# Masked attention layer on one core: exponentials and sums of four heads at a time, three denominator terms, transposes moved, batches written out

## The reference

```python
h = jnp.maximum(_layernorm(x, axis=-1), 0.0)          # x: 8 x 1024 x 512
q = heads(h @ Wq + bq); k = heads(h @ Wk + bk); v = heads(h @ Wv + bv)   # 16 heads of 32
scores = jnp.einsum('bhqd,bhkd->bhqk', q, k) / sqrt(32)
scores = jnp.where(adj[:, None] == 0, -jnp.inf, scores)
attn = jax.nn.softmax(scores, axis=-1)
out = jnp.einsum('bhqk,bhkd->bhqd', attn, v).transpose(0, 2, 1, 3).reshape(8, 1024, 512)
return x + out @ Wo + bo
```

## Time and profile before

| | |
|---|---|
| median of 3 runs | 2086.7 us (2085.78 to 2088.95) |
| profiled execution, its own time / its span | 2085.51 / 2083.6 us |
| TensorE busy | 1932.5 us, 93% |
| VectorE busy | 1557.3 us, 75% |
| ScalarE busy | 1478.1 us, 71% |
| POOL busy | 1302.1 us, 62% |
| granted TensorE clock, mean | 0.989 |
| DMA | 206.61 MB, mean 99 GB/s, the program's queue 35.2% of 16 engines |

### The profile page before, as it was taken

The page is one execution under the profiler, slowest core; times in us unless marked ns, Lnnn a source line. Parts: engine busy times, 40 slices in busy tenths (PEclk is TensorE's granted clock), DMA queues, the critical chain, the costliest instruction groups (busy, mean ns, idle before and its releaser), DMA issues.

```text
span 2083.6 us, 40441 instructions
## 1 busy us (share of the span) xinstructions
PE 1932.5 (93%) x14336; PEld 776.5 (37%) x14336; DVE 1557.3 (75%) x1587; ACT 1478.1 (71%) x1765; POOL 1302.1 (62%) x581
## 2 busy tenths in 40 slices
PE   3799899998999999999999999999899998999977
PEld 2334344343344333443334333334333343444312
DVE  5688777878768787687867877778767787767773
ACT  3577786677867788668876778767777677866672
POOL 0377567556666567656667557666557566676574
PEclk8999999999999999999999999999999999999999
DMA  5433244342444324343351434424234332442302
GB/s 177 122 87 96 82 112 132 88 107 64 120 112 124 83 76 132 86 122 86 92 142 56 115 93 117 119 74 119 81 109 122 88 106 66 117 122 64 74 1 81
DMA packets 103222, 206.61 MB, mean 99 GB/s; under 512 B 11616, under 2 KB 11744, under 8 KB 103008
## 3 DMA queue, kind: packets, MB, share of 16 engines
q1 hardware_dynamic: 103008, 203.80, 35.2%
HBM read 153.43 MB, written 50.33 MB: 98 GB/s over the span
## 4 chain that ended last, share of the span: by engine, by line
PE 76%; DVE 7%; issue 6%; DMA 5%; ACT 2%; POOL 1%; SPq 1%; DVEq 0%; ACTq 0%; POOLq 0%
PE ps L694 20%; PE ps L681 19%; PE ps L654 15%; PE ps L705 10%; PE ps L668 7%; PE ps L661 6%; DVE ring L905 4%; DMA k_stack<-k_parts 2%; DMA k_parts<-k_part 1%; SPq L513 1%; DMA edges<-adjT 1%; ACT hT_hi L776 1%; DVE k_part L918 1%; POOL acc L1079 1%; ACT ring L770 1%
## 5 line engine op out<-in xcount | busy, mean ns | idle before, releaser
L905 DVE TENSOR_TENSOR ring<-ps,mask 128x1024 f32<-128x1024 f32 x1024 | 1234.6, 1219 | 435.7 <-PE ps L681 399.9
L770 ACT ACTIVATE ring<-ring 128x1024 f32<-128x1024 f32 x1024 | 1069.7, 1051 | 382.9 <-DVE ring L905 374.6
L1079 POOL TENSOR_TENSOR acc<-ring 128x1024 f32<-128x1024 f32 x256 | 604.1, 2371 | 730.2 <-ACT ring L770 729.4
L681 PE MATMUL ps<-q_stack,k_stack 128*128 128x512 f16 x2048 | 610.4, 382 | 85.2 <-DVE ring L905 61.4
L1079 POOL TENSOR_TENSOR acc<-acc,ring 128x1024 f32<-128x1024 f32 x256 | 617.6, 2432 | 0.0
L694 PE MATMUL ps<-ring,v_sb 128*32 128x512 f32 x4096 | 509.1, 604 | 0.0
L681 PEld LDWEIGHTS ps<-q_stack,k_stack 128*128 128x128 f16 x2048 | 157.1, 98 | 481.8 <-DVE ring L905 246.4
L694 PEld LDWEIGHTS ps<-ring,v_sb 128*32 128x32 f32 x4096 | 100.9, 109 | 252.3 <-issue 218.1
L705 PE MATMUL ps<-acc,ones 128*32 128x512 f32 x1024 | 139.8, 597 | 2.7 <-issue 2.6
L705 PE MATMUL ps<-ring,ones 128*32 128x512 f32 x1024 | 137.3, 592 | 0.0
L661 PE MATMUL ps<-wv_hi,hT_hi 128*128 128x128 f16 x1024 | 103.1, 219 | 3.2 <-DVE k_part L918 3.2
(11 more groups left out here) (80 smaller groups left out, 1593.4 us busy)
## 6 DMA issues: line engine op xcount, KB each, us to landing
x_in<-x SPq DMA_DIRECT2D x168, 256.0 KB, 2.7
edges<-adjT SPq DMA_DIRECT2D x128, 256.0 KB, 2.9
q_stack<-q_parts SPq DMA_DIRECT2D x128, 256.0 KB, 4.9
k_stack<-k_parts SPq DMA_DIRECT2D x128, 256.0 KB, 5.0
q_parts<-q_part SPq DMA_DIRECT2D x32, 512.0 KB, 2.7
k_parts<-k_part SPq DMA_DIRECT2D x32, 512.0 KB, 2.9
out<-x_in SPq DMA_DIRECT2D x56, 256.0 KB, 2.1
ring<-x SPq DMA_DIRECT2D x2, 1024.0 KB, 6.6
```

Of the source, the lines that this page charges most:

```text
L681: i = nc.tensor.matmul(ps_s(j)[:, hh, :], stack["k"][:, up % 2, h, kt * P:(kt + 1) * P], stack["q"][:, up % 2, h, half * HALF:(half + 1) * ...
L770: nc.scalar.activation(tile, tile, ACT.Exp, scale=SCALE / UP / UP).then_inc(s["prob_ready"], 1)
L905: nc.vector.tensor_tensor(ring[:, slot_of(kt, pair), :].rearrange("p (a n) -> p a n", n=HALF), ps_s(j), mask[:, kt:kt + 1, half * HALF:(ha ...
L1079: nc.gpsimd.tensor_tensor(acc[:, group, pair, :], first_of, ring[:, slot_of(kt, pair), :], ALU.add).then_inc(s["sum_done"], 1)
```

## The change

Five things are done at once.

1. Exponentials: `exp` does nothing for the first tile of a pair and takes both tiles, 128 x 2048, at the second.
2. Sums: POOL adds 128 x 2048 at a time. Group A is now key tiles 0 to 3, group B 4 to 6: five adds in a sweep, at key tiles 1, 2, 3, 5 and 6. Each add within a group waits for the add before it.
3. Denominators: three terms, A, B and d7. BLOCKS has them at other places: nothing at tile 16 (the next sweep's 0), and p6, dB, p7, d7 all at 18 (the next sweep's 2).
4. Chunks: T_AT is gone. The transposes stand in the lists, t0 to t3 between the chunks of unit 2 and t4 to t7 between those of unit 3, and everything is spread over SLOTS, which now has tile 16. In both units the order is q0, k0, v0 and then q1, k1, v1. Laid out, k's second chunk ends at tile 23 in unit 2 (before 11), at 24 in unit 3 (before 20), and at 21 in unit 1 (before 23).
5. Batches 1 to 6 are written out as straight code on all five engines.

```diff
-BLOCKS = {6: ("p0", "p1"), 10: ("p2", "p3", "dA"), 14: ("p4", "p5"), 16: ("p6", "dB", "d6"), 18: ("p7", "d7")}
-TERMS = "AB67"
+BLOCKS = {6: ("p0", "p1"), 10: ("p2", "p3"), 14: ("p4", "p5", "dA"), 18: ("p6", "dB", "p7", "d7")}
+TERMS = "AB7"
+
+SUMMED = {1: 0, 2: 1, 3: 2, 5: 3, 6: 4}
+SUMS = 5
+SUMMED_AT = {"A": 3, "B": 5}
...
-NORMALISE_AT = {(2, 5): 0, (2, 7): 1, (2, 9): 2, (2, 11): 3, (2, 23): 4, (2, 25): 5, (2, 27): 6, (2, 29): 7}
-T_AT = {(2, 19): 0, (2, 21): 1, (2, 23): 2, (2, 25): 3, (2, 27): 4, (2, 29): 5, (3, 1): 6, (3, 3): 7}
-SLOTS_OF = [SLOTS, SLOTS, [j for j in SLOTS if j <= 17], [j for j in SLOTS if j >= 5]]
-NORMS_AT = [29, 29, 18, 29]
+NORMALISE_AT = {(2, 5): 0, (2, 7): 1, (2, 9): 2, (2, 11): 3, (2, 21): 4, (2, 25): 5, (2, 29): 6, (3, 2): 7}
+NORMS_AT = 29
...
     if up == UNITS - 1:
-        return [] if last else ts + PROJ + [NORMS]
+        return [] if last else [q[0], ts[4], k[0], *ts[5:8], v[0], q[1], k[1], v[1], NORMS]
     if up == 2:
-        return PROJ + [NORMS] + ts
+        if last:
+            return [q[0], k[0], v[0], q[1], k[1], v[1], NORMS]
+        return [q[0], k[0], v[0], ts[0], q[1], ts[1], k[1], ts[2], v[1], ts[3], NORMS]
...
             graph(0, True, False)
-            with pe.Fori(1, B - 1) as b:
+            for b in range(1, B - 1):
                 graph(b, False, False)
...
             def exp(U, j):
-                half, r = divmod(j, SWEEP)
+
+                kt, pair = divmod(j % SWEEP, PAIRS)
+                if pair != PAIRS - 1:
+                    return
                 act.wait_ge(s["score_masked"], U * TILES + j + 1)
-                tile = ring[:, slot_of(*divmod(r, PAIRS)), :]
+                tile = ring[:, slot_of(kt, 0):slot_of(kt, 0) + PAIRS, :]
                 nc.scalar.activation(tile, tile, ACT.Exp, scale=SCALE / UP / UP).then_inc(s["prob_ready"], 1)
...
-                if kt < RING_KT:
-                    if not very_first:
-                        if kt < 2:
-                            dve.wait_ge(s["pv_done"], 8 * V + kt - 3)
-                            dve.wait_ge(s["sum_done"], 8 * V + 2 * kt - 3 + pair)
-                        else:
-                            dve.wait_ge(s["den_done"], len(TERMS) * V + kt - 3)
-                else:
-                    dve.wait_ge(s["pv_done"], 8 * V + kt - 3)
-                    dve.wait_ge(s["sum_done"], 8 * V + {4: 1, 5: 1, 6: 3, 7: 5}[kt] + pair)
+                before = (V - 1, kt + QT - RING_KT) if kt < RING_KT else (V, kt - RING_KT)
+                if not (kt < RING_KT and very_first):
+                    W, k = before
+                    dve.wait_ge(s["pv_done"], QT * W + k + 1)
+                    if k == QT - 1:
+                        dve.wait_ge(s["den_done"], len(TERMS) * (W + 1))
+                    else:
+                        dve.wait_ge(s["sum_done"], SUMS * W + SUMMED[k if k in SUMMED else k + 1] + 1)
...
-            def sums(U, j, very_first):
-                half, r = divmod(j, SWEEP)
-                kt, pair = divmod(r, PAIRS)
+            def sums(U, half, kt, very_first):
                 V = U * SWEEPS + half
-                group, k = divmod(kt, 3)
-                pool.wait_ge(s["prob_ready"], U * TILES + j + 1)
-                if k == 1 and pair == 0 and not very_first:
+                group, n = kt // 4, SUMS * V + SUMMED[kt]
+                pool.wait_ge(s["prob_ready"], V * QT + kt + 1)
+                begins = kt % 4 == 1
+                if begins and not very_first:
                     pool.wait_ge(s["den_done"], len(TERMS) * (V - 1) + group + 1)
-                if k == 2:
-                    pool.wait_ge(s["sum_done"], 8 * V + 4 * group + pair + 1)
-                first_of = ring[:, slot_of(kt - 1, pair), :] if k == 1 else acc[:, group, pair, :]
-                nc.gpsimd.tensor_tensor(acc[:, group, pair, :], first_of, ring[:, slot_of(kt, pair), :], ALU.add).then_inc(s["sum_done"], 1)
+                if not begins:
+                    pool.wait_ge(s["sum_done"], n)
+                tile = ring[:, slot_of(kt, 0):slot_of(kt, 0) + PAIRS, :]
+                first_of = ring[:, slot_of(kt - 1, 0):slot_of(kt - 1, 0) + PAIRS, :] if begins else acc[:, group]
+                nc.gpsimd.tensor_tensor(acc[:, group], first_of, tile, ALU.add).then_inc(s["sum_done"], 1)
```

More of the change, by code:

```diff
@@ L879, in _ @@
             graph(0, True, False)
-            with act.Fori(1, B - 1) as b:
+            for b in range(1, B - 1):
                 graph(b, False, False)
@@ L1040, in _ @@
             graph(0, True, False)
-            with dve.Fori(1, B - 1) as b:
+            for b in range(1, B - 1):
                 graph(b, False, False)
@@ L1099, in graph @@
                                     bias_x(b, first, b - 1, t)
-                        if j % SWEEP // PAIRS in (1, 2, 4, 5):
-                            sums(U, j, first and up == 0 and j < SWEEP)
+                        half, r = divmod(j, SWEEP)
+                        kt, pair = divmod(r, PAIRS)
+                        if pair == PAIRS - 1 and kt in SUMMED:
+                            sums(U, half, kt, first and up == 0 and half == 0)
             pool.wait_ge(s["const_loaded"], 16 * 6)
             graph(0, True, False)
-            with pool.Fori(1, B - 1) as b:
+            for b in range(1, B - 1):
                 graph(b, False, False)
```

95 lines of the change are left out of this document (41 added, 54 removed).

## The result

| | before | after |
|---|---|---|
| median of 4 runs, us | 2087.82 (2085.78 to 2091.12) | 2204.66 (2200.73 to 2208.41) |
| ratio, 95% interval | | 1.0558 (1.0532 to 1.0584): slower |
| profiled execution / its span, us | 2085.51 / 2083.6 | 2208.41 / 2206.6 |
| granted TensorE clock, mean | 0.989 | 0.964 |

The forecast was 2079, with 2045 to 2122 as its range. The result, 2205, is 117 us slower than before and lies outside. The five parts cost more than any of the rivals had them cost.

What follows compares the result with a forecast made beforehand. A ring of waits through POOL's sums was to bind the light units at 28.9 us a sweep, TensorE unit 1. Batch and end terms totalled -7.8 on 2085.5, giving 2077.7; with 1.2 for the median, 2079, range 2045 to 2122.

Steps and rivals of the forecast that it cites:

- The adds: POOL's sums of 2048 elements: 4.54 us each, bounds 4.49 and 4.74.
- The ring: Reciprocal, exponential of key tile 1, POOL's five sums, dB and d7 wait in a circle: 28.9 us a sweep in light units.
- the sign that I had named: If right, 28.9 us from logarithm to logarithm in units 2 and 3.
- Unit 0's first sweep: 28.9 us plus 1.0 and four bias adds of 1.25 between POOL's sums: 34.9 us.
- Written out: The loop's jump back goes five times, 3.3 us each: 17 us saved with the tails, longer program costed at nothing.
- Fewer terms and empty tiles: TensorE: one denominator term fewer, -1.9 us a unit; tiles with nothing but scores, +1.1 at each of 31 unit borders.
- This makes ScalarE lighter by ... 100 us, worth nothing by itself: ScalarE is 2% of the chain: Exponentials of 2048 at 1.9 us each on ScalarE: 100 us less work, no time gained by itself.
- Such a pair of adds took 5.70 us instead of 4.70 ... +1.0 in each unit but unit 1.: First sweep of a unit: VectorE's low part of the attention output falls on a POOL add, +1.0 us except unit 1.
- I count some 14 us from k's end to the next unit against 12.5 ... 0, bounds 0 and 2 per unit.: Ends of units 2 and 3: k's later end was to cost no wait for the k stack, with 1.1 us slack.
- Bank waits ... 0.4 in unit 2: q, k and v waiting for banks behind the short transposes: 0.4 us in unit 2, bounds 0 and 1.8.
- B: Rival: POOL adds of 4.74 us between key tiles 1 and 6 slow the ring, 2128 us; chance 0.18.
- A: Rival: TensorE stays the bound because the ring opens, batch 239.7 us, whole 2009 us; chance 0.12.

Runs made afterwards that it cites:

- a_recip: The changed kernel with ScalarE's reciprocal one tile later, behind the exponential of key tile 1: 2172.46 us.
- b_longexp: b_unroll with exponentials of 2048 only, POOL's eight adds of 1024 kept: 2135.95 us.
- b_long: b_unroll with exponentials and adds of 2048, four adds a sweep, four terms, old chunks: 2165.57 us.
- b_longadd: b_unroll with the four adds of 2048 only, exponentials of one pair kept: 2096.23 us.
- a_olow: The changed kernel with the attention output of units 2 and 3 split at tiles 17 and 19, in POOL's pause, not 5 and 7: 2166.11 us.
- b_long_olow: b_long with the output split of units 2 and 3 moved as in a_olow: 2127.60 us.
- b_chunks16: b_unroll with the new chunk order and slots alone, four terms, pieces of 1024: 2171.14 us.
- b_unroll: The kernel before with batches 1 to 6 written out as straight code, nothing else: 2074.64 us.
- a_kfirst: The changed kernel with q1 and k1 before v0 in unit 3, so k ends at tile 20 instead of 24: 2209.80 us.
- b_three: b_unroll with three terms at their new places and ten adds of 1024, exponentials of 1024, old chunks: 2041.92 us.
- b_best: b_three with the moves of a_recip and a_olow: 2031.07 us.

## Why the prediction was wrong, step by step

**Right.** The adds: 4.54 forecast, 4.563 measured for those that open a group, 4.549 in a_recip; the Trainium skill's 4497 ns for 2048 elements ("GPSIMD Engine Reference", section 3.1) agrees within 1.5%. The ring: from the logarithm in unit 1's second sweep to the one in unit 2's first it took 29.2 us in every batch, 28.9 forecast, and opening it brought 32 us, net of the low part's shift. But the sign that I had named, 28.9 from logarithm to logarithm in units 2 and 3, did not show: from there on these stretches took 30.8 to 38.6 us in batches 1 to 6, so other waits were added to the ring there or took its place. Unit 0's first sweep took 34.9 between its logarithms, as forecast; but b_longexp has 67.5 us for its unit 0 without that ring, so unit 0's sum is no proof of its working. Written out: -13 for -17, with the jump's 3.3 us right and unit 2's low part against it. Fewer terms and empty tiles: -0.8 a unit forecast, 25 in all, -33 measured; some of the difference is unit 2's low part again, which is luck.

**"This makes ScalarE lighter by ... 100 us, worth nothing by itself: ScalarE is 2% of the chain"** is the step that failed most. I priced a merged instruction by its busy time and asked whether its engine was the bound. It has a second price: whatever stands behind it in order starts up to 0.9 us later, and I looked for that at one place, the first half of a key tile. It also holds for the high parts of transposes and for every conversion of a chunk, and VectorE's masking queues behind those. By itself that costs 61 us (b_longexp); the long adds cost 22 by themselves.

**"Such a pair of adds took 5.70 us instead of 4.70 ... +1.0 in each unit but unit 1."** I read the meeting of low part and sum off POOL's row. The row of VectorE stood in the same group of rows, with 1.35 us, and was one of the harmless ones: before, this line had 1341 ns in the median, but 3482 at most. VectorE's instruction is held until POOL's running add is over, so what it costs depends on the length of that add: up to 4.7 us with adds of 2048 (5.03 in b_long, 5.29 in b_longadd), 3.5 with 1024. And whether it meets one at all changes with shifts of 0.05 us. By a_olow it is up to 39 us in units 2 and 3, by b_long_olow 38 (both with ScalarE's high part moved along), where the sum had 1.0 for each of these 16 units. The Trainium skill ("GPSIMD Engine Reference", section 1) says that the two engines share their SBUF interfaces and contend when a VectorE instruction has two SBUF inputs, which this one has; the traces agree.

**"I count some 14 us from k's end to the next unit against 12.5 ... 0, bounds 0 and 2 per unit."** In the fourth batch k's last product ended at 1096.9 (a start of 1096.32 and 0.59). The unit was over 11.8 us later (1108.7), because its light last tiles run faster than the ring's pace; and the scores could start 16.8 us later (1113.7), for the store was issued after 4.1 us and took 12.7 to the scores, not 10.7. Short by 5.0, and TensorE waited 5.3. Both halves of a small margin were off, and the bound of 2 was not tried against them. b_chunks16 shows the wait without anything else of the change. Its gap at the batch's end is 6.6 us longer than b_unroll's, 46 of its 96 us in seven batches; the 2.4 us by which each following unit 0 grew, part of it at 1.2 GHz, may belong to it too. What is the stack's own in the changed kernel stays open, since a_kfirst turned up another wait instead.

**"Bank waits ... 0.4 in unit 2"**, and none for unit 3: in unit 3 k0 waited 1.9 us for q0's low part behind the short t4 (at 1056.53). A chunk's bank is free only when the one two before it has been split, and a short transpose between two chunks leaves less time for that. The larger cost of t4's place, the 4.8 us between the maskings of tiles 6 and 7 (1.1 in b_unroll), was in no term at all.

**The clock was in no term.** 157.6 us at 1.2 GHz against 44.4. In batches 1 to 6 of the changed kernel, the two units 2 with none of it took 62.2 us; those with 3.4 to 6.8 us of it took 64.1 to 65.5. Time at half the clock can lose at most half of itself, 1.7 us of 3.4, and most of these units are longer by more than that: the clock is only a part of the difference, and the waits that stand before it are another. So the 113 us more of such time are at most 56 of the 117 us. This bound is only argued: no run changes the clock alone, and the figure isn't added to the parts above, since each part's own measurement holds its share of it.

**The rivals.** B had the right sign and the wrong place: it wanted adds of 4.74 us, and even its 2128 is 77 too fast. A was the mistaken way to think of the changed kernel. With short pieces it comes closer: b_three has units of 66.3, 59.7, 61.6 and 56.1 us where A had 65.4, 60.2 and twice 57, so all but unit 2 are within 1 us, and b_best's 2031 stands 22 above A's 2009. The three terms were the good part of this change, and all of the rest but the written-out batches took it away. Having found one ring that closed at 28.9 us, I took it for the bound of every unit and added the rest as small terms, without following the places in unit 3 where something was newly in front of something else.

## What to carry to other kernels

An engine far from being the bound can still be the one whose instruction lengths matter: before two instructions are merged, list what stands behind the merged one on its queue, and who waits for that. A merge that saves 100 us of ScalarE cost 61 us of time here. Read a meeting of two engines from both of their rows, and take the maximum of the row, not its usual value, if the change doubles what it waits behind. And when a sum has a margin of about a microsecond, price the case that it is missed: at the batch border that brought a wait of 5.3 us, with a stretch at half the clock behind it. And when versions are compared, look first whether such a meeting came or went between them: in b_unroll it moved by 0.05 us and cost 1.2 us in each unit 2.
